# B times delta u of one pair in eight by way of ScalarE and TensorE, and all C pairs on GpSimd, in a fused macaron kernel

## The reference

```python
x, z = jnp.split(xz, 2, axis=-1)                 # (4, 2048, 1024) each
x = _silu(conv_general_dilated(x, conv_w, ...) + conv_b)
Bm, Cm = jnp.split(x @ W_x, 2, axis=-1)          # 16 states each
delta = jax.nn.softplus(x @ W_dt + b_dt)

def step(h, t):                                  # _selective_scan, over 2048 tokens
    delta_t, B_t, C_t, u_t = t
    dA = jnp.exp(delta_t[:, :, None] * A[None, :, :])
    dBu = delta_t[:, :, None] * B_t[:, None, :] * u_t[:, :, None]
    h = dA * h + dBu
    y = jnp.einsum('bds,bs->bd', h, C_t)
    return (h, y)

out = ((y + x * D) * _silu(z)) @ W_out
```

## Time and profile before

| | us |
|---|---|
| median of three runs (lowest, highest) | 5179.13 (5176.7, 5179.95) |
| the profiled execution's own time | 5180.01 |
| its span in the trace | 5178.2 |
| first scan of chunk 0 to the end of the last chunk's steps, in the trace | about 712 to 4556 |

### The profile page before, as it was taken

How to read it: one execution, slowest core, us unless ns; L and a number is a source line. 1 busy time by engine, 2 the same in 40 slices (tenths; PEclk the granted TensorE clock), 3 DMA queues, 4 the chain that set the end, 5 groups by cost and what they waited for, 6 DMA issues and landing times. The chain is left out here.

```text
span 5178.2 us, 79404 instructions
## 1 busy us (share of the span) xinstructions
PE 4693.1 (91%) x23936; PEld 3776.5 (73%) x23936; DVE 4584.5 (89%) x7668; ACT 3753.9 (72%) x9592; POOL 3878.2 (75%) x1637
## 2 busy tenths in 40 slices
PE   8999988898888988898899888888988989789999
PEld 6778767777777777777777777777777777668887
DVE  6777669999999999999999999999999999977775
ACT  5656557888787888888788887878888788744443
POOL 1111059999999999999999999999999999931110
PEclk9999999999999999999999999999999999989999
DMA  3222231111111111111111111111111111111111
GB/s 84 89 83 75 109 106 43 52 46 46 54 58 54 50 46 46 46 46 46 50 55 46 46 54 56 56 50 46 46 46 46 46 46 47 65 61 49 66 57 41
DMA packets 137375, 291.88 MB, mean 56 GB/s; under 512 B 23280, under 2 KB 40688, under 8 KB 136944
## 3 DMA queue, kind: packets, MB, share of 16 engines
q1 hardware_dynamic: 136944, 286.75, 16.4%
HBM read 218.53 MB, written 68.18 MB: 55 GB/s over the span
## 5 line engine op out<-in xcount | busy, mean ns | idle before, releaser
L977 POOL TENSOR_TENSOR mx_dbu<-mx_bs,mx_du 128x2048 f32<-128x2048 f32 (+1 forms) x513 | 2327.2, 4537 | 120.9 <-DVE mx_hp L1276 120.6
L1193 ACT ACTIVATE mx_ps_da<-mx_dl,mx_a 128x256 f32<-128x256 f32 x4096 | 1776.3, 465 | 99.0 <-DVE mx_hp L1276 61.6
L1276 DVE TENSOR_TENSOR_SCAN mx_ps_da<-mx_ps_da,mx_hst,mx_dbu 128x256 f32<-128x256 f32 x2016 | 1405.5, 737 | 125.1 <-ACT mx_ps_da L1193 106.9
L1276 DVE TENSOR_TENSOR_SCAN mx_hp<-mx_ps_da,mx_hst,mx_dbu 128x256 f32<-128x256 f32 x1568 | 1145.6, 731 | 11.5 <-ACT mx_ps_da L1193 11.5
L995 POOL TENSOR_TENSOR mx_hp<-mx_hp,mx_cs 128x1024 f32<-128x1024 f32 (+1 forms) x512 | 1069.4, 2095 | 1.3 <-ACT mx_hst L1117 1.3
L1396 PE MATMUL mx_ps_m<-mx_u,mx_w_dt 128*128 128x256 f32 x4096 | 930.8, 381 | 2.7 <-issue 2.7
L1396 PEld LDWEIGHTS mx_ps_m<-mx_u,mx_w_dt 128*128 128x128 f32 x4096 | 762.9, 191 | 95.7 <-issue 3.3
L1378 PE MATMUL mx_ps_m<-mx_hT,mx_w_in 128*128 128x256 f32 x2048 | 554.0, 417 | 279.7 <-DVE mx_u L1254 279.4
L1289 DVE TENSOR_TENSOR mx_hc<-mx_ps_da,mx_cs 128x512 f32<-128x512 f32 x1024 | 683.5, 667 | 2.8 <-issue 1.9
L1378 PEld LDWEIGHTS mx_ps_m<-mx_hT,mx_w_in 128*128 128x128 f32 x2048 | 395.9, 203 | 389.8 <-DVE mx_u L1254 330.5
L1426 PEld LDWEIGHTS mx_ps_y<-mx_ident,mx_hp 128*128 128x128 f32 x3584 | 444.5, 143 | 321.5 <-POOL mx_hp L995 174.8
(11 more groups left out here) (126 smaller groups left out, 7440.4 us busy)
## 6 DMA issues: line engine op xcount, KB each, us to landing
mx_bs<-bc_scratch SPq DMA_DIRECT2D x128, 512.0 KB, 4.3
mx_cs<-bc_scratch SPq DMA_DIRECT2D x128, 512.0 KB, 3.7
mx_hT<-hT_scratch SPq DMA_DIRECT2D x32, 518.0 KB, 4.1
hT_scratch<-f_h2T SPq DMA_DIRECT2D x16, 1024.0 KB, 8.9
mx_xo<-xs_scratch SPq DMA_DIRECT2D x32, 512.0 KB, 3.7
x_scratch<-mx_xo SPq DMA_DIRECT2D x32, 512.0 KB, 2.9
f_x<-in_L_attn_inp SPq DMA_DIRECT2D x12, 1024.0 KB, 6.5
xs_scratch<-f_x SPq DMA_DIRECT2D x12, 1024.0 KB, 4.3
```

Of the source, the lines that this page charges most:

```text
L977: G.tensor_tensor(dbu[:, n % NM:n % NM + k].rearrange("p n s t -> p (n s) t"), bs[:, g:g + k].rearrange("p n s t -> p (n s) t"), bcast(du[ ...
L1193: ins = A.activation(ps_da[DA_BANK[p]][:, k, :], dl[:, b % NL, :], ACT.Exp, scale=a_sb[:, b, s:s + 1])
L1276: ins = V.tensor_tensor_scan(da if in_psum(p) else hp[:, n % NH, k, :], da, dbu[:, n % NM, s, :], 0.0 if first else hst[:, b, SG * g + s:S ...
```

## The change

One pair in eight (half 0 of the third step of every block, `on_pe`, p = 8b + 4) gets its B times delta u another way. TensorE turns `du` of the block to token-major order into the block's `ps_m` bank (two transposes, `turn_du`, at n % 4 = 3). There B of a token is one number per partition, so ScalarE multiplies with it as a scale, out of PSUM into `dbuT` (four instructions of 128x128, `turned_du_times_b`, at n % 4 = 0, behind the first tap and ahead of the decay of half 1). TensorE turns the products back into the PSUM bank of that pair (four transposes, `turn_dbu`, at n % 4 = 1). The pair's decay goes to a tile of SBUF instead (`da_sb`), one half step earlier, and the scan reads decay from SBUF and the product from PSUM, and writes its states over the product. The delta product two blocks ahead, which takes the same `ps_m` bank, waits until ScalarE has read the turned `du`.

GpSimd's `times_b` skips this pair: every second instruction has 1536 columns instead of 2048. SyncE loads B once more per chunk as columns (`load_bT`, two DMAs of 256 numbers). `ALL_IN_PSUM` is empty: VectorE's `times_c_second` goes, and GpSimd multiplies the second pair of all 32 steps by C.

```diff
@@ -805,7 +812,12 @@
         EARLIEST = IN_AT[0]
 
         DA_BANK = [p % NA for p in range(2 * NU - 1)] + [1]
-        ALL_IN_PSUM = (4, 5, 20, 21)
+        ALL_IN_PSUM = ()
+        ON_PE = 2
+        S_PE = SG * ON_PE
+        DU_TURN_AT = [NG * b - 1 for b in range(ND)]
+        DU_TIMES_B_AT = [NG * b for b in range(ND)]
+        DBU_TURN_AT = [NG * b + ON_PE - 1 for b in range(ND)]
         NE = len(ALL_IN_PSUM)
 
         def in_psum(p):
@@ -845,6 +857,14 @@
 
         def y_sum(b):
             return ps_y[b % 2][:, 0:T]
+
+        def on_pe(p):
+
+            return p % 2 == 0 and p // 2 % NG == ON_PE
+
+        def du_bank(c, b):
+
+            return ps_c if isinstance(c, int) and c == LAST and b >= ND - 2 else ps_m[b % 2]
 
         def m_bank(b):
             return ps_m[b % 2]
@@ -882,6 +902,12 @@
                 sp.wait_ge(s_bc, 16 * (i + 1))
                 sp.dma_start(bc_dram[:, :], bc[:, :]).then_inc(s_bcd, 16)
 
+            def load_bT(par):
+
+                for k in range(SD):
+                    sp.dma_start(bT[:, par, k, :], bc_dram[S_PE + k, :].rearrange("(j p) -> p j", p=P),
+                                 allow_slow_non_contiguous=True).then_inc(s_bt, 16)
+
             def store_out(i):
 
                 sp.wait_ge(s_o, TJ * (i + 1))
@@ -974,9 +1002,10 @@
                     pool.wait_ge(s_du, ND * i + b + 1)
                 if not (is0(i) and n < NM):
                     pool.wait_ge(s_sc, 2 * NU * i + 2 * (n - NM + 2))
-                G.tensor_tensor(dbu[:, n % NM:n % NM + k].rearrange("p n s t -> p (n s) t"),
-                                bs[:, g:g + k].rearrange("p n s t -> p (n s) t"),
-                                bcast(du[:, b % 2, :], k * SG), ALU.mult).then_inc(s_m1, k)
+                skip = SD if on_pe(2 * n) else 0
+                G.tensor_tensor(dbu[:, n % NM:n % NM + k].rearrange("p n s t -> p (n s) t")[:, skip:, :],
+                                bs[:, g:g + k].rearrange("p n s t -> p (n s) t")[:, skip:, :],
+                                bcast(du[:, b % 2, :], k * SG - skip), ALU.mult).then_inc(s_m1, k)
 
             def times_c(c, n):
 
@@ -1107,6 +1136,29 @@
             def log(c, b):
                 act.wait_ge(s_en, ND * c + (b + 1))
                 A.activation(en[:, b % 2, :], en[:, b % 2, :], ACT.Ln, bias=1.0).then_inc(s_sp, 1)
+
+            def turned_du_times_b(c, cp, b):
+
+                act.wait_ge(s_dut, ND * c + (b + 1))
+                if not (is0(c) and b == 0):
+                    act.wait_ge(s_db, ND * c + b)
+                if b == 0:
+                    act.wait_ge(s_bt, 16 * SD * (c + 1))
+                for k in range(SD):
+                    for j in range(TJ):
+                        ins = A.activation(dbuT[:, k, j, :], du_bank(c, b)[:, j * P:(j + 1) * P], ACT.Copy,
+                                           scale=bT[:, cp, k, j:j + 1])
+                ins.then_inc(s_duc, 1)
+
+            def decay(i, p):
+
+                n, half = divmod(p, 2)
+                b, g = divmod(n, NG)
+                dst = da_sb if on_pe(p) else ps_da[DA_BANK[p]]
+                for k in range(SD):
+                    s = SG * g + SD * half + k
+                    ins = A.activation(dst[:, k, :], dl[:, b % NL, :], ACT.Exp, scale=a_sb[:, b, s:s + 1])
+                ins.then_inc(s_da, 1)
 
             def keep(c, n):
 
@@ -1184,14 +1236,14 @@
                         act.wait_ge(s_dl, ND * i + b + 1)
                     for half in range(2):
                         p = 2 * n + half
-                        if in_psum(before(p)):
+                        if on_pe(p):
+                            pass
+                        elif in_psum(before(p)):
                             keep_psum(i, p)
+                            decay(i, p)
                         else:
                             bank_scanned(i, p)
-                        for k in range(SD):
-                            s = SG * g + SD * half + k
-                            ins = A.activation(ps_da[DA_BANK[p]][:, k, :], dl[:, b % NL, :], ACT.Exp, scale=a_sb[:, b, s:s + 1])
-                        ins.then_inc(s_da, 1)
+                            decay(i, p)
                         if half == 0:
                             for bb, s in due(DT_AT, n, i, RELU):
                                 relu(i + s, bb)
@@ -1200,6 +1252,10 @@
                             for bb, s in due(YT_AT, n, i):
                                 copy_y(i + s, bb)
                                 skip(i + s, (par + s) % 2, bb)
+                            for bb, s in due(DU_TIMES_B_AT, n, i):
+                                turned_du_times_b(i + s, (par + s) % 2, bb)
+                    if on_pe(2 * n + 2):
+                        decay(i, 2 * n + 2)
                     if n >= KEEP_LAG:
                         keep(i, n - KEEP_LAG)
                     elif not is0(i):
@@ -1272,8 +1328,14 @@
                 if k == 0:
                     dve.wait_ge(s_da, 2 * NU * i + (p + 1))
                 s = SD * half + k
-                da = ps_da[DA_BANK[p]][:, k, :]
-                ins = V.tensor_tensor_scan(da if in_psum(p) else hp[:, n % NH, k, :], da, dbu[:, n % NM, s, :],
+                bank = ps_da[DA_BANK[p]][:, k, :]
+                if on_pe(p):
+                    if k == 0:
+                        dve.wait_ge(s_db, ND * i + b + 1)
+                    da, db = da_sb[:, k, :], bank
+                else:
+                    da, db = bank, dbu[:, n % NM, s, :]
+                ins = V.tensor_tensor_scan(bank if in_psum(p) else hp[:, n % NH, k, :], da, db,
                                            0.0 if first else hst[:, b, SG * g + s:SG * g + s + 1], ALU.mult, ALU.add)
                 if k == SD - 1:
                     ins.then_inc(s_sc, 1)
@@ -1392,6 +1454,8 @@
 
                 pe.wait_ge(s_zc, ND * c + (b + 1))
                 pe.wait_ge(s_u, ND * (c + 1))
+                if not (is0(c) and b < 2):
+                    pe.wait_ge(s_duc, ND * c + (b - 1))
                 for k in range(ND):
                     ins = M.matmul(m_bank(b)[:, 0:T], w_dt_sb[:, k, b * P:(b + 1) * P], u[:, cp, k, :],
                                    start=(k == 0), stop=(k == ND - 1))
@@ -1428,6 +1492,29 @@
                                        skip_group_check=True)
                 return ins
 
+            def turn_du(c, b):
+
+                if isinstance(c, int) and c == LAST and b >= ND - 2:
+                    pe.wait_ge(s_o, TJ * LAST)
+                    if b == ND - 1:
+                        pe.wait_ge(s_duc, ND * LAST + b)
+                else:
+                    pe.wait_ge(s_zc, ND * c + (b + 3))
+                pe.wait_ge(s_du, ND * c + (b + 1))
+                for j in range(TJ):
+                    ins = M.transpose(du_bank(c, b)[:, j * P:(j + 1) * P], du[:, b % 2, j * P:(j + 1) * P], ident[:, :])
+                ins.then_inc(s_dut, 1)
+
+            def turn_dbu(c, b):
+
+                n = NG * b + ON_PE
+                pe.wait_ge(s_duc, ND * c + (b + 1))
+                pe.wait_ge(s_sc, 2 * NU * c + (2 * n - 2))
+                for k in range(SD):
+                    for j in range(TJ):
+                        ins = M.transpose(ps_da[DA_BANK[2 * n]][:, k, j * P:(j + 1) * P], dbuT[:, k, j, :], ident[:, :])
+                ins.then_inc(s_db, 1)
+
             def sum_psum_states(c, n):
 
                 b, g = divmod(n, NG)
@@ -1479,6 +1568,10 @@
                         k = LAST_OUT_AT.index(n)
                         for j in range(TJ):
                             last_out_product(j, range(2 * k, 2 * k + 2))
+                    for b, s in due(DU_TURN_AT, n, i):
+                        turn_du(i + s, b)
+                    for b, s in due(DBU_TURN_AT, n, i):
+                        turn_dbu(i + s, b)
                     for part, s in due(OUT_AT, n, i):
                         if isinstance(i, int) and i + s == LAST:
                             continue
```

More of the change, by code:

```diff
@@ L726, in mixer_phase @@
         yt = sb("yt", [P, 2, T])
+        da_sb = sb("da_sb", [P, SD, T])
+        dbuT = sb("dbuT", [P, SD, TJ, P])
+        bT = sb("bT", [P, 2, SD, TJ])
         ps_y = [ctx.enter_context(nc.psum_tensor(f"mx_ps_y{n}", [P, 512], F32)) for n in range(2)]
@@ L757, in mixer_phase @@
         s_m1 = sem("dbu_ready")
+        s_dut = sem("du_turned")
+        s_duc = sem("turned_du_times_b")
+        s_bt = sem("b_columns_loaded")
+        s_db = sem("dbu_in_psum")
         s_da = sem("da_ready")
@@ L900, in chunk @@
                 sp.wait_ge(s_bcd, 16 * (i + 2))
+                load_bT(1 - par)
                 for g in range(NG):
@@ L917, in _ @@
             sp.wait_ge(s_bcd, 16)
+            load_bT(0)
             for g in range(NG):
@@ L1458, in prologue @@
             def prologue():
+                pe.wait_ge(s_id, 2)
                 for n in range(EARLIEST, 0):
+                    for b, c in due_before(DU_TURN_AT, n):
```

(2 more changed lines are left out.)

## The result

The changed kernel takes 5248.65 us (median; 5247.91 to 5249.85) against 5179.54 before: ratio 1.0133, 95% interval 1.0117 to 1.0149. It is slower by 69 us; forecast were 81, and 5260 us.

A forecast was written before the change was run, and what follows sets the result against it. VectorE's list was taken as the bound. Silus -0.7, GpSimd -0.5, step 16 +3.2 and step 28 +0.6 gave +2.6 us per chunk, +81 us over 31 chunks: 5260 us, range 5180 to 5330.

The forecast's parts named there:

- VectorE sets the pace and the bound moves to TensorE's chain at step 16: VectorE's list is the bound; after the change it waits for ScalarE's decay at step 16, +3.2 us per chunk.
- The chain: TensorE, delta product of step 12 to input product of step 15: nothing hides the new wait; input product +2.18 us.
- Copies: ScalarE's four scaled 128x128 copies per block: 0.3 us each, 1.2 us a block, between 0.12 and 0.41 each.
- Silus: -0.7: Steps 5, 6, 21 and 22: of VectorE's 2.35 us saved, only 0.35 is won, twice a chunk.
- Moved and added without cost: Copies at other blocks, early decay, scans reading both memories and B column loads: taken as 0.
- Step 28: +0.6: First tap of step 28 waits for TensorE: +0.6 us a chunk, between 0 and +1.5.
- The clock rival: TensorE's clock falls in the long chain of steps 12 to 15: +4.35 us a chunk, 5314 us, chance 15%.
- GpSimd: -0.5: GpSimd's list becomes 4.3 us shorter, below VectorE's: -0.5 us per chunk, between 0 and -0.9.
- The sum: Per chunk -0.7 - 0.5 + 3.2 + 0.6 = +2.6 us, over 31 chunks +81 us, 5260 us.
- Faster by relief: Delta product's wait hidden, VectorE's list 2.35 us shorter and GpSimd's share 0.5: -2.9 a chunk, 5089 us, chance 13%.
- New PSUM reads: VectorE could turn out bound by its scans' new PSUM reads: 0.1 us a scan, 1.6 a chunk; no chance given.
- no difference: Copies at 0.12 us, step 28 clean, silus giving all: about 0 a chunk, 5180 us, chance 7%.

The follow-up runs named there:

- experiment 1: Changed kernel with the last three out parts moved from steps 14, 15 and 18 to 16, 18 and 20: 5154.74 us, ratio to before 0.9948.
- experiment 2: Kernel before the change with only its last three out parts moved to steps 16, 18 and 20: 5168.61 us, ratio 0.9978.
- experiment 4: Changed kernel with copies for only the first of the pair's two states, the second state's own product left out: 5190.66 us, ratio 1.0016.
- experiment 5: Changed kernel with ScalarE's copies ahead of the first tap and only two of the four copies made: 5163.29 us, ratio 0.997.
- experiment 6: Changed kernel with two of four copies, ahead of the first tap, and TensorE's turn back of the product behind the out part: 5145.96 us, ratio 0.9933.
- Experiment 8: Kernel before the change with only ALL_IN_PSUM emptied, so GpSimd multiplies all 32 steps' second pairs by C: 5179.5 us, ratio 0.9996.
- experiment 9: Changed kernel with copies ahead of the first tap and the last three out parts at steps 16, 18 and 20: 5127.19 us, ratio 0.9899.

## Why the prediction was right

- *VectorE sets the pace and the bound moves to TensorE's chain at step 16.* Right, and shown by experiments 1 and 2. Forecast were +3.2 us. VectorE waits 2.84 us there in chunk 14, and step 16 takes 3.04 over the undisturbed 4.30 in the mean; but it grew by 2.54 only, since it took 4.81 before. The row of 12.8 us shown above is that wait: in 12 of 28 chunks VectorE stood there already, and chunk 14, the only one I read, is not among them.
- *The chain.* Its times came within 0.22 us. I put 1.5 of the 2.18 us on the delta product's wait for the copies, and noted that the scans of step 12 would just be over when the turn back of `dbuT` starts. Both hold: the turn starts 4.31 us into step 12 (2475.76), directly behind the sums. What I missed is how little then hangs on the copies. Experiments 4 to 6 show that the turn back, queued ahead of out part and gate product, would wait for those scans until 4.08 us into the step anyway. With the turn where it is, only 0.2 us hang on the copies there (with the 0.5 of two copies ahead of the decay, about the 0.66 of experiment 4); once it is moved, the delta product's start counts. The lower end of my range, +1.8 with copies of 0.12 us, let them count twice; with this limit the same sum gives about +2.2.
- *Copies.* 0.3 us each assumed; four run in 1.14 us and the next instruction starts 1.00 after the first, 0.25 each.
- *Silus: -0.7.* Too much. The sum over ScalarE's list gave -0.35 twice; measured were -0.24 for steps 5 and 6 and +0.11 for 21 and 22. At steps 20 and 21 ScalarE has other work, and the copies, costed at nothing, lengthen it: without half of them step 22 loses 0.36 us.
- *"Moved and added without cost."* Wrong by +0.85 us in the steps that hold the copies and +0.29 in step 14. The medians of steps 8, 12 and 28 did not move (4.32 us), so there it is some chunks that pay, and I had read only chunk 14. In step 14 VectorE's product waits for TensorE's transposes of an earlier one, 7.1 us in 17 waits between 1000 and 4360 us: TensorE's lateness shows there too. The B columns cost nothing: their DMAs landed in 2.1 us, and no engine is shown waiting for them.
- *Step 28: +0.6.* It was +0.10. ScalarE's first tap of step 28 waited for TensorE in 24 of 28 chunks before and in 3 after, and before none of it reached VectorE. The clock rival fell: 0.99 is granted, not less.
- *GpSimd: -0.5.* Somewhat small: step 31 alone gave -0.62, and of steps 3, 15 and 19 (-0.36 together) the last two had held waits for `dbu`, 3 in 28 chunks each, of which none is left.
- *The sum.* 3.2 + 0.6 - 0.7 - 0.5 = 2.6 against 2.49, and this closeness is luck. Against their terms step 16, step 28 and GpSimd's steps came out 1.6 us lower; the silus and the small steps costed at nothing came out 1.6 us higher. The large term alone, 3.2 against 2.54, is what the mechanism earned. The whole run became 69 us longer and not 81 mainly because the first two and last two chunks together added nothing.
- *Rivals.* Faster by relief: the relief was there, 281 us of waiting on GpSimd, and won the 0.6 us of step 31 while the chain took 2.5. New PSUM reads: scans of that kind take 742 ns, the others 746 and 751. The sum of "no difference" has a slip: GpSimd's 0.5 stands in it as a loss; as a gain it makes -1.05 a chunk, and no longer about 0.
- *Not run:* the new way of B times delta u by itself, with `ALL_IN_PSUM` left as before. Experiment 8 shows that the C part alone changes nothing, not that the two parts add up.

## What to carry to other kernels

When an operation is queued on an engine that runs ahead of the bound one, look at what it waits for, not only at its length. The four transposes take 0.44 us, but they tie TensorE to the current scans at the one place where it had no slack: the out part behind them can't start before 4.08 + 0.44 us into step 12, where it had started 2.78 us into it. That is 1.7 us, even for a delta product as early as before. This is worked out; what was run is experiment 6, where moving them behind the out part won 0.81 us from delta to gate product and 17 us of the run. Find the fullest stretch of such an engine before adding to it, and look first whether work due elsewhere can leave it: taking two output parts out of that stretch turned a loss of 1.3% into a gain of 0.5%. Relief of an engine that is busy but not waited for is worth what its waits are, here 0.6 us a chunk.

## What the runs showed of the hardware

TensorE had more work and a higher clock. The granted clock over the whole run is 0.986 against 0.972 before, and the lower level of 1.2 GHz was granted for 143 us instead of 293. Before, TensorE's idle time lay mostly in front of the gate product, in 135 waits of 1.8 us in the mean; after, it lies mostly ahead of the delta products, in 214 waits of 1.0 us in the mean, 0.91 us in chunk 14 and 3.2 at most. In the two kernels without the change's work on TensorE (2 and 8) the clock stayed at 0.971 and 0.975. Neither the work nor the waits ahead of one product order all the runs: in experiment 9 TensorE has the same work as in the changed kernel and waits only 75 us ahead of the delta products, and yet the clock is 0.979, with 215 us at the lower level. Why the change raised the clock stays open.
